# Keys stored in pair order, value blocks in two parts, half statistics ahead, routing steps reordered, another engine awaiting the scatters

## The reference

```python
# cross attention: 1601 context rows and the 64 new rows are the keys and values
q, k_new, v_new = x_norm @ wq.T, x_norm @ wk.T, x_norm @ wv.T
k, v = concat([ctx, k_new]), concat([ctx, v_new])
x = x + (softmax(q @ k.T / 32) @ v) @ wo.T
# self attention: 16 heads of 64, rotary embedding, causal
x = x + attn(layernorm(x), w_qkv, w_out)
# mixture of 8 experts: weights from sigmoid(x_norm @ Wr), most tokens use few experts
x = x + sum_e weight_e * ((silu(x_norm @ Wg_e) * (x_norm @ Wu_e)) @ Wd_e)
```

## Time and profile before

| | us |
|---|---|
| median of 3 runs (lowest, highest) | 1290.64 (1289.09, 1295.51) |
| profiled execution | 1296.42 |
| its span, first to last instruction | 1294.6 |
| PE busy | 1215.7 (94%) |
| DVE busy | 819.7 (63%) |
| ACT busy | 633.6 (49%) |
| mean granted TensorE clock | 0.975 |

### The profile page before, as it was taken

One profiled execution on the slowest core, in us unless ns is written; L12 is line 12 of the kernel. 1 busy time (PEld: TensorE's weight loads), 2 busy tenths in 40 slices (PEclk: granted clock), 3 DMA queues, 4 the chain that ended last, 5 costly groups with the idle time before them and its releaser, 6 DMA issues.

```text
span 1294.6 us, 19218 instructions
## 1 busy us (share of the span) xinstructions
PE 1215.7 (94%) x7762; PEld 1061.1 (82%) x7762; DVE 819.7 (63%) x1026; ACT 633.6 (49%) x604; POOL 95.8 (7%) x74
## 2 busy tenths in 40 slices
PE   4999999999998999999997599999999999999996
PEld 3887777777777888888886598989899999999894
DVE  7335788988998547464566474746565565656464
ACT  4113788888897423114543244444444445454440
POOL 0011000000000000000000011121111111121201
PEclk9999999999999899999999699998999999999998
DMA  8254889999999544220244176765766767676632
GB/s 296 97 179 150 299 324 366 366 362 360 381 368 328 180 177 163 98 98 33 94 152 168 51 258 193 229 207 171 216 207 221 214 208 211 216 215 225 192 131 33
DMA packets 46872, 272.98 MB, mean 211 GB/s; under 512 B 5880, under 2 KB 6024, under 8 KB 18528
## 3 DMA queue, kind: packets, MB, share of 16 engines
q1 hardware_dynamic: 36768, 243.48, 51.8%
q0 software_dynamic: 10048, 28.71, 9.2%
HBM read 255.92 MB, written 16.25 MB: 210 GB/s over the span
## 4 chain that ended last, share of the span: by engine, by line
PE 79%; DVE 7%; ACT 5%; issue 4%; DMA 4%; POOL 0%; SPq 0%; ACTq 0%; DVEq 0%; POOLq 0%
PE ps L1404 21%; PE ps L1405 21%; PE ps L1406 21%; PE ps L1501 6%; DVE lo L932 4%; DMA out<-y,target 3%; ACT hi L625 3%; PE ps L1614 2%; PE ps L1865 1%; PE ps L1549 1%; PE ps L1514 1%; ACT scores L687 1%; PE ps L1707 1%; PE ps L1691 1%; PE ps L1418 0%
## 5 line engine op out<-in xcount | busy, mean ns | idle before, releaser
L932 DVE TENSOR_TENSOR lo<-raw,hi 128x2048 fp32r<-128x2048 f32 (+1 forms) x198 | 443.5, 2252 | 171.7 <-ACT hi L625 169.4
L625 ACT ACTIVATE hi<-raw 128x2048 fp32r<-128x2048 f32 (+1 forms) x198 | 370.5, 1881 | 263.8 <-PE ps L1406 254.9
L1404 PE MATMUL ps<-act_hi,hi 128*128 128x240 f32 (+1 forms) x1216 | 359.3, 296 | 10.9 <-DVE act_lo L955 4.8
L1406 PE MATMUL ps<-act_hi,lo 128*128 128x240 f32 (+1 forms) x1216 | 360.0, 296 | 0.0
L1405 PE MATMUL ps<-act_hi,hi 128*128 128x240 f32 x1024 | 284.4, 278 | 0.0
L1404 PEld LDWEIGHTS ps<-act_hi,hi 128*128 128x128 f32 x1216 | 232.2, 191 | 21.1 <-DVE h_lo L1373 5.2
L1406 PEld LDWEIGHTS ps<-act_hi,lo 128*128 128x128 f32 x1216 | 232.6, 191 | 7.8
L1405 PEld LDWEIGHTS ps<-act_hi,hi 128*128 128x128 f32 x1024 | 195.3, 191 | 0.3
L1404 PE MATMUL ps<-hi,act_hi 128*128 128x512 f32 x320 | 126.2, 394 | 0.0
L1406 PE MATMUL ps<-hi,act_lo 128*128 128x512 f32 x320 | 124.8, 390 | 0.0
L1405 PE MATMUL ps<-lo,act_hi 128*128 128x512 f32 x320 | 124.6, 389 | 0.0
(11 more groups left out here) (228 smaller groups left out, 1449.6 us busy)
## 6 DMA issues: line engine op xcount, KB each, us to landing
raw<-weights SPq DMA_DIRECT2D x124, 1024.0 KB, 5.0
raw<-keys SPq DMA_DIRECT2D x36, 1024.0 KB, 5.5
raw<-context SPq DMA_DIRECT2D x31, 1024.0 KB, 7.5
raw_more<-context SPq DMA_DIRECT2D x17, 1024.0 KB
raw_more<-keys SPq DMA_DIRECT2D x12, 1024.0 KB
xq<-x_in SPq DMA_DIRECT2D x4, 512.0 KB, 6.5
raw_more<-weights SPq DMA_DIRECT2D x4, 512.0 KB
new_keys_t<-kvs POOLq DMA_DIRECT2D x8, 256.0 KB, 3.2
```

Of the source, the lines that this page charges most:

```text
L625: act.activation(part(hi, k, kind), part(raw, k, kind), ACT.Copy).then_inc(hi_done, 1)
L932: dve.tensor_tensor(part(lo, k, kind), part(raw, k, kind), part(hi, k, kind), ALU.subtract).then_inc(lo_done, 1)
L1404: pe.matmul(out, a_hi, b_hi, start=first, stop=False)
L1406: return pe.matmul(out, a_lo, b_hi, start=False, stop=last)
```

## The change

Seven edits:

1. A value block is two units now, `("block", 0, f)` and `("block", 1, f)`: each loads 128 x 512 (0.25 MB), is split as such, and gives 12 of the 24 matmuls. They stand behind u = 2 and u = 4 of the keys stretches 0 and 1 (blocks 0 and 1) and behind u = 1 and u = 3 of the values stretches 0 to 5 (blocks 2 to 7). The list grows from 120 to 128 units.
2. The host stores the keys so that the score columns come in pair order; `turn_weights` reads contiguous columns.
3. The bn_stats of the first half rows of all four tiles are issued between the two splits that precede `add_and_norm`; `moments` does only the second half there.
4. ACT's small Exp stands between `logits_copy(0)` and `logits_copy(1)`.
5. `split(U_FFN + 2)` stands behind the Exp steps on ACT and behind `slot_values()` on DVE.
6. POOL waits for `meta` and reads it ahead of the last expert's scatters, and no longer waits for the scatters.
7. SP waits for all scatters as its last instruction.

```diff
-            if u == (4 if what == "keys" else 2) and extra:
-                yield "block", None, next(blocks)
-    units = list(stretch("keys", 0, True))
+            if u in places:
+                yield "block", places.index(u), f
+    units = list(stretch("keys", 0, (2, 4)))
     for s in range(B):
         if s + 1 < B:
-            units += stretch("keys", s + 1, s < 6)
-        units += stretch("values", s, s == 0)
+            units += stretch("keys", s + 1, (2, 4) if s == 0 else ())
+        units += stretch("values", s, (1, 3) if s < 6 else ())
...
-            unit("block_ready", u + 1)
+            unit(*(("block_ready", u + 1) if b == 1 else (None, 0)))
...
+            sp.wait_ge(scattered, 64 * NE + 16)
...
                 if e + 1 < NE:
                     gather(e + 1)
+                else:
+                    pool.wait_ge(meta_ready, 1)
+                    more = pool.value_load(meta[0:1, 0:1], min_val=0, max_val=MORE)
                 scatter(e)
-            pool.wait_ge(scattered, 64 * NE + 16)
-            pool.wait_ge(meta_ready, 1)
-            more = pool.value_load(meta[0:1, 0:1], min_val=0, max_val=MORE)
...
                     logits_copy(0)
+                    act.activation(small[:, 14, 29:30], eps[:, :], ACT.Exp).then_inc(y_done, 1)
                     logits_copy(1)
...
-            split(U_FFN + 2)
-            act.activation(small[:, 14, 29:30], eps[:, :], ACT.Exp).then_inc(y_done, 1)
...
             act.activation(small[:, 6, :], small[:, 4, :], ACT.Exp, scale=-1.0 / 0.3).then_inc(edist_ready, 1)
+            split(U_FFN + 2)
...
-                    moments(t)
+                    moments(t, first=1)
...
             split(U_QKV)
+            for t in range(TT):
+                dve.wait_ge(evacuated, O_WO + t + 1)
+                half_stats(t, 0)
             split(U_QKV + 1)
...
-                    columns = bass.ds(2 * P * (kc // 2) + kc % 2, P, step=2) if kc < 12 else slice(KFULL, KV)
+                    columns = slice(kc * P, (kc + 1) * P) if kc < 12 else slice(KFULL, KV)
...
-                for c in range(C):
-                    at = slice(c * P, (c + 1) * P)
+                for c in range(4 * h, 4 * h + 4):
+                    at = slice((c - 4 * h) * P, (c - 4 * h + 1) * P)
```

More of the change, by code:

```diff
@@ L39, in attention_units, with stretch @@
     blocks = iter(range(C))
-    def stretch(what, b, extra):
+    def stretch(what, b, places):
+        f = next(blocks) if places else None
         for u in range(7):
             yield what, b, u
-            if u == (4 if what == "keys" else 2) and extra:
-                yield "block", None, next(blocks)
-    units = list(stretch("keys", 0, True))
+            if u in places:
+                yield "block", places.index(u), f
+    units = list(stretch("keys", 0, (2, 4)))
     for s in range(B):
         if s + 1 < B:
-            units += stretch("keys", s + 1, s < 6)
-        units += stretch("values", s, s == 0)
+            units += stretch("keys", s + 1, (2, 4) if s == 0 else ())
+        units += stretch("values", s, (1, 3) if s < 6 else ())
     assert next(blocks, None) is None
@@ L445, in load_values, with load_block @@
                     load(k, ctx_d[b, KFULL:KV, :], dst=raw_of(k)[0:KREM, 0:D])
-            def load_block(k, f):
-                load(k, w_d[W_V + f // 2, :, (f % 2) * D:(f % 2 + 1) * D], dst=raw_of(k)[:, 0:D])
+            def load_block(k, f, h):
+                at = (f % 2) * D + h * HALF
+                load(k, w_d[W_V + f // 2, :, at:at + HALF], dst=raw_of(k)[:, 0:HALF])
             for t in range(TT):
@@ L465, in _ @@
                 else:
-                    load_block(U_KEYS0 + n, u)
+                    load_block(U_KEYS0 + n, u, b)
             for k in range(RING):
@@ L576, in part @@
             if kind == BLOCK:
-                return whole[:, 0:D]
+                return whole[:, 0:HALF]
             return whole
@@ L583, in blocks_before @@
         def blocks_before(n):
-            return sum(what == "block" for what, _, _ in ATTENTION[:n])
+            return sum(what == "block" and h == 1 for what, h, _ in ATTENTION[:n])
         def tail_parts(buf, k):
@@ L747, in attention @@
                     split(U_KEYS0 + n + AHEAD)
-                    if n > 0 and ATTENTION[n - 1][0] == "block":
+                    if n > 0 and ATTENTION[n - 1][0:2] == ("block", 1):
                         block_copy(ATTENTION[n - 1][2])
@@ L933, in split, with half_stats, moments @@
                                   ALU.subtract).then_inc(lo_done, 1)
-            def moments(t):
-                for h in range(2):
-                    steps.done(dve.bn_stats(stats[:, t, h, :], x[:, t, h * HALF:(h + 1) * HALF]))
+            def half_stats(t, h):
+                steps.done(dve.bn_stats(stats[:, t, h, :], x[:, t, h * HALF:(h + 1) * HALF]))
+            def moments(t, first=0):
+                for h in range(first, 2):
+                    half_stats(t, h)
                 steps.wait()
@@ L1179, in _ @@
             split(U_FFN)
+            for t in range(TT):
+                dve.wait_ge(evacuated, E_WOUT + t + 1)
+                half_stats(t, 0)
             split(U_FFN + 1)
             add_and_norm(2, E_WOUT, O_WOUT, lambda t: t % 2)
-            split(U_FFN + 2)
             def sm(j):
@@ L1569, in late, with value_block @@
                 ins.then_inc(late_ready, 1)
-            def value_block(f, k):
-                if f == 0:
+            def value_block(f, h, k):
+                if h == 0 and f == 0:
                     pe.wait_ge(evacuated, O_QK + 16)
-                else:
+                elif h == 0:
                     pe.wait_ge(block_copied, f)
                 unit_ready(k)
-                for c in range(C):
-                    at = slice(c * P, (c + 1) * P)
+                for c in range(4 * h, 4 * h + 4):
+                    at = slice((c - 4 * h) * P, (c - 4 * h + 1) * P)
                     ins = three(ps[:, BLOCK_BANK, :], hi[:, k % RING, at], lo[:, k % RING, at],
                                 act_hi[:, c, :], act_lo[:, c, :], c == 0, c == C - 1)
-                ins.then_inc(block_ready, 1)
+                ins.then_inc(block_ready if h == 1 else unit_used, 1)
             def turn_block(f, s):
@@ L1626, in attention @@
                     if what == "block":
-                        value_block(u, k)
+                        value_block(u, b, k)
                     elif what == "keys":
@@ L1965 @@
     context = g["ctx_2048"]
-    keys = context[:, :KFULL].reshape(B, 3, HALF, 2, 4, P).transpose(0, 1, 3, 5, 4, 2).reshape(B, 6, P, UNIT)
+    in_pairs = context[:, :KFULL].reshape(B, 6, P, 2, D).transpose(0, 1, 3, 2, 4).reshape(B, KFULL, D)
+    keys = in_pairs.reshape(B, 3, HALF, 2, 4, P).transpose(0, 1, 3, 5, 4, 2).reshape(B, 6, P, UNIT)
     tail = context[:, KFULL - 1:].reshape(B, KTAIL, C, P).transpose(0, 3, 2, 1)
```

## The result

| | before | after |
|---|---|---|
| median of 18 runs each (lowest, highest), us | 1292.76 (1289.09, 1299.59) | 1286.81 (1279.08, 1291.72) |
| profiled execution, its span, us | 1296.42, 1294.6 | 1289.46, 1287.6 |
| mean granted clock | 0.975 | 0.973 |

The ratio is 0.9953, with a 95% interval of 0.9937 to 0.9969: 6.1 us faster, between 4 and 8. The forecast was 12.4. The sign was right, the size was half.

A forecast was written before the change was run, and what follows sets the result against it. In the cross attention no engine alone was the bound; the value block on PE kept DMA (floor 182.4 of 192.03 us) and DVE from theirs. -7.5 - 4 + 3.0 + 1.95 + 0 - 4.5 - 1.3 = -12.4, from 1290.6 to 1278.2; range 1271 to 1288.

The forecast's parts named there:

- Block in halves, five periods: Cross attention, values stretches: half blocks end ACT's 3.55 us stall for PE, gaining 1.5 a period, 7.5 us in all.
- loads the floor all along: Rival, chance 0.23: the five periods take the same time whatever PE does; 1289.8 us, no change.
- less ahead: Rival, chance 0.08: half blocks fill whole tiles, so fewer bytes are on the way and the queue runs dry; 1305.7 us, slower.
- Pair order at nothing: Keys in pair order: same bytes, same matmuls, a small matmul's 0.1 us isn't waited for; no gain or loss.
- Handover: From attention to `wo`: turned landing tiles make the first `wo` load late, so PE waits; 3.0 us lost, bounds 0 and 4.7.
- 1.7 if this gap pulls the clock down: Behind the gap at `wo`: 1.7 us more lost if the clock falls for 4 us; only in the upper bound.
- The opening: Start of the cross attention: a half block fills PE's 2.5 us gap before the first turning of weights; 4 us gained, bounds 0 and 8.7.
- attention: Five periods of the cross attention: 7.5 us gained by half blocks, bounds 0 and 9.6.
- Statistics ahead: Norms 1 and 2: four bn_stats delay the first tile, PE waits 1.3 us at each; 0.65 gained before routing, net 1.95 lost.
- Routing: Before the gather: DVE starts on the logits at 705.6 instead of 710.13, 4.5 us saved; the moved table load is covered.
- The end: Last scatters and closing DRAIN: last scatter 2.7 us later, but DRAIN overlaps the landing; 1.3 us gained, ±1.7 possible.
- it can begin when POOL has issued: POOL's closing DRAIN, 5.2 us long, begins at 1287.5 before the scatters land and ends at 1292.7, 1.7 us less than 1294.4.

The follow-up runs named there:

- halves_no_pairs: The changed kernel with the pair order of the keys undone, half blocks kept: 1286.28 us, ratio 0.9953 against the kernel before.
- old_tiles: The changed kernel with the landing tiles of the attention's units turned by four, so the first `wo` units find free tiles: 1277.59 us, ratio 0.9899 against the kernel before.
- whole_blocks: The changed kernel with value blocks whole and in their old places, all other edits kept: 1283.28 us, ratio 0.9935 against the kernel before.
- pairs_alone: The kernel before with only the pair order of the keys added: 1288.85 us, ratio 0.9973 against the kernel before.
- gap_filled: The changed kernel with 14 extra unread matmuls on PE between the last context unit and the first `wo` matmul: 1284.24 us, ratio 0.9939 against the kernel before.
- meta_behind: The changed kernel with POOL reading `meta` behind the last four scatters instead of ahead of them: 1278.02 us in one run.
- routing_back: The changed kernel with the small Exp and the third expert unit's split back ahead of the routing steps: 1291.40 us, ratio 0.9987 against the kernel before.

## Why the prediction was off, point by point

- **Block in halves, five periods: right by its number.** 7.1 for 7.5, and ACT's stalls for PE are gone (under 1 us ahead of their splits in the five periods, for 17.7). The bound behind it did not hold: I took 0.95 x 192.03 = 182.4 for the time that the DMA engines need, and expected a share near 1.00 at 184.5. The share was 0.96, which makes 177.4, with halves_no_pairs the same and the whole blocks at 183. So the busy time of the DMA engines isn't fixed by the bytes here, and that 1.5 a period came out next to this floor was in part luck. The rival "loads the floor all along" is out (184.7 against 191.9), and so is "less ahead".
- **Pair order at nothing: the reason was wrong.** "The 0.1 us or so of a small matmul" looked at the matmul, not at its weight load, which is 1.50 against 0.88 for twelve. That it cost the sum of the five periods nothing is because the halves had already taken PE off the path. The Trainium skill (TensorE: Matmul & The Clock Gate, LDWEIGHTS) has the load's time follow the number of columns, the same 128 in both; here the measurement decides, the step counts.
- **Handover: the gap right, the step behind it mis-sized.** I took 3.0 and kept "1.7 if this gap pulls the clock down" as a bound. It did, for 7 us, costing 2.7 (old_tiles against after, 37.55 and 40.25). In the seven profiles with the gap the clock was low behind it each time, for 7 us in three and for 3.5 in four, where it cost 1.4 to 1.7; so the bound had the size of the mild case. The same text had shown in the earlier trace rows that a gap of 2.5 does this; the term should have been in the sum. This is the largest failed step: a cost kept out of the sum, of 1.4 to 2.7 us.
- **The last period: a step that was missing.** PE comes sooner to a late piece, and DVE, left behind, makes it wait 2.52 instead of 0.95, at times with the clock behind it. Both edits share in that: with pair order alone the wait is 1.6 (whole_blocks, pairs_alone), with halves alone 1.24 (halves_no_pairs), with both 1.9 to 2.9. +2.3 in this execution, -0.3 to +1.8 in the others with these tiles. The prediction never asked what becomes of the stretch behind the last half block.
- **The opening: right place, mis-sized.** -1.9 for -4 here, -2.2 to -2.6 in six further kernels that, like the one before, began it at the lower clock. Where it began at full clock it took 69.0 to 69.1 with halves (old_tiles, gap_filled, meta_behind) and 71.45 without (pairs_alone): -2.4 too. I counted the filled gap as 2.5 gained. It isn't: PE still idles 1.50 ahead of the half block (143.74, for DVE's `lo`), the turning is now queued behind that block and came at 30.68 instead of 28.84, and what is gained lies in the first period, 40.59 for 44.33.
- **Statistics ahead: both waits right** (1.04 each for 1.3). The gain ahead of routing was 0.5 for 0.65 by the landmark.
- **Routing: right**, 4.45 for 4.5, in the trace and by undoing it; the table load cost nothing.
- **The end: the sign right, the size small.** The last scatter is 2.8 later against ACT's last y (4.32 for 1.54), as predicted (2.7). The failed step is "it can begin when POOL has issued" and then takes 5.2: that would end 6.8 behind the last scatter's start, and it ended 8.2 behind. The DRAIN was 11.0 us long and ended 2.6 behind the landing. SP's wait gains 3.0 and the order behind `meta` gives 2.8 of it back; meta_behind keeps the first alone. What the DRAIN waits for stays open.

By terms, forecast to measured: opening +2.1, attention +0.4, last period +2.3, `wo` clock +2.6, end +1.1, others +0.2; 8.7 in all, which takes -12.4 to -3.7 for these stretches in the profiled pair. The runs say -6.1 with an interval of 4 to 8; the remainder is spread between executions, mostly stretches at the low clock that come and go, and was not settled. The losses at `wo` and in the last period have one cause, a PE gap with a low clock behind it; I had priced that cause at one place, as a bound, and nowhere else. Because of it the terms of single executions move by 1 to 3 us, so this sum by terms holds for the profiled pair.

## What to carry to other kernels

Price a gap on PE of 2 us or more at the gap and, with a chance, at what the clock takes behind it, half of the time at the lower level. Take the chance from several executions, as one trace may show either case. Look for such gaps wherever an edit turns a ring of buffers or takes slack away; filling one with unread matmuls tests this in one run. Ask of a stationary operand how its columns are stepped, not only how many there are. A big edit and a small one in the same stage can gain the same microseconds: undo each alone before crediting either.

## What the runs showed of the hardware, unexpected

- Twelve weight loads of 128 float32 columns on 64 partitions: 1.50 us with a step of 2, 0.88 without, at the same granted clock.
- Whether a PE gap of 2 to 3 us was followed by 1.2 GHz depended on the place more than on its length. Unfilled, over the fourteen profiles: ahead of `wo` (2.9 to 3.4) in 7 of 7, for 3.5 or 7 us; ahead of the turning of sample 6's output (2.14) in 13 of 13, for 10 or 14 us, where PE does small matmuls behind the gap; ahead of the first turning of weights (2.6) in 4 of 4, for 3.5 or 7 us; ahead of the first score unit (2.55) in 10 of 14; at a late piece (1.9 to 2.9) in 4 of 10, with the clock full behind 2.90 in gap_filled and low behind 1.88 in routing_back. What decides at the last two was not tried.
- POOL's closing DRAIN ended 2.6 us behind the landing of the last indirect scatter, whether it began 2.8 ahead of that scatter's start (11.0 us long) or 1.1 behind (6.6); begun behind the landing it took 5.2. Why was not tried.
